# A decoder layer of 32 tiles on one core: second buffers for the front's packs, small scales on GpSimd, TensorE kept busy ahead of the weights, and new instruction orders

## The chip, the cores and the metric

One NeuronCore of a Trainium2 chip runs the kernel. The metric is the device time of one execution in microseconds (us); the number to compare is the median of several executions. TensorE (PE in the profile) multiplies, VectorE (DVE), ScalarE (ACT) and GpSimd (POOL) do the rest, and the sync engine (SP) issues the DMAs. Each engine runs its own instruction list in order and waits for the others through semaphores.

## What is computed

The reference is one decoder layer on x of 32 x 128 x 256 with a context of the same shape, each of the 32 sequences being one tile:

```python
x = _layernorm(x + _L0_attn_ref(x, Wq, bq, Wk, bk, Wv, bv, Wo, bo, orf))
x = _layernorm(x + _L0_xattn_ref(ctx_1024, x, ctx_1024, xWk, xWq, xWv))
x = _layernorm(x + _L0_ffn_ref(x, w_gate, w_up, w_down))
```

The first attention is linear, with 16 heads of 16: phi(z) = (exp(z orf^T / 16^0.25 - |z|^2 / 8) + 1e-6) / 8, kv = phi(k)^T v, out = phi(q) kv / (phi(q) sum phi(k)), and then the output projection. The second is softmax attention of the tile's x over its context, with 16 x 16 matrices shared by the heads. The FFN (256 to 1024 to 256, silu gate) quantizes activations to 8 bits by row and weights to the three values -1, 0, 1 by matrix.

## The kernel before, in words

Every tile passes through about 70 steps, each a small function with the tile number t. A step waits for its producers, issues one to 32 instructions and counts up its own semaphore. The steps, in the order of the data:

- Front: load_x; xhi and xlo (GpSimd, L468 to L474) split x into two fp16 parts in xpk; xTp transposes them; xT copies them out of PSUM; qkm and vm project with passes of 512 and 256 columns (L1355); qk and v (VectorE, L969 to L981) add the biases; sq, nf, nr form the norms; hi (ScalarE, L676), lo (GpSimd, L501), nhi and nlo (L483 to L489) fill pkA, an fp16 pack that the DMA transposes qT and kT turn into pkAT; phq0, phq1, phk0, phk1 and the exponentials behind them give the features.
- Linear attention: kvs, vsm, kve, kvp, kvm, nump, nT, ntp, rd, at, aTp, aT, wo, ad1, and the layer norm bs1, y1, rs1, x1.
- Second attention: chi and clo pack the context in pkC, transposed by cT; x1Tp, x1T, tm, thi, tlo fill pkT, transposed by tT; s0 and s1 (L1587, L1596) give scores, m0 and m1 the row maxima, mTp, mT and the DMA `row` put them into the operand; st0, st1, p0, p1, pv0, pv1, oxT, oxp, rx, oxn, ya2 and the layer norm bs2, y2, rs2, x2.
- FFN: am, ac, ar, qnt, xqf quantize; xqTp, xqT, g0, g1, u0, u1; th0, th1, gl0, gl1, hu0, hu1, hh0, hh1, hx, hc, hr, hs scale; hm0, hm1, hq0, hq1 quantize, the DMA transpose hqT; dn, ad3, and the layer norm bs3, y3, rs3, ot, store.

A layer norm ends in `rstd` (L510) on GpSimd: ve, nm, a power, nmr, each on 128x1. `sg` (L1091) and `sd` (L1147) on VectorE form three scales of 128x1: sgate and sprod from acl, sdown from hcl.

The tiles are software-pipelined: in iteration i an engine issues each of its steps for tile i minus the step's lag. The order of the steps within an iteration is written out by hand for each engine, in `iteration(i, par)`; par is the parity of the tile and picks the buffer where there are two. `ramp` holds the same steps as tiles enter (each with its first index and the tile it stops at), with the preparation of the FFN weights in between (`once`), `drain` the same as tiles leave. Both are straight code; two iterations and then a compiled loop of two iterations per turn stand between them (`run`, L306), so that tiles 14 to 29 pass the front in the loop. Where two steps share a PSUM bank, a wait for an unrelated step (`wait_looped`, `only_at`) keeps them apart. xpk, xT, qk, pkA, pkAT, phk, x1T, pkC, pkT, hq and hqT have one buffer, which gives waits such as these:

```python
wait_ahead(pool, t, par, ("nr", 0), landings=(("kT", -1), ("qT", -1),))   # nhi, L484
wait_moved(act, "kT", t, par, -1)                                         # hi, L677
wait(dve, "lo", t, -1)                                                    # qk_, L972
```

The FFN weights are loaded by SP (load_gate, load_up, load_down, 1 MB each). `magnitudes` (L941) sums their absolute values on VectorE, `ffn_means` adds over the partitions on TensorE, `ffn_scales` and `scaled` (L958, L961) scale them, `signed` (L659) takes signs, and `transpose_ffn` and `evacuate_ffn` bring them into place.

Of the kernel before, what the change touches and what calls it, by code (L numbers as in the profile page):

```python
# [14 lines left out]
H = 16  # L15
# [14 lines left out]
def decoder_kernel(nc: bass.Bass, x, ctx_in, Wq, bq, Wk, bk, Wv, bv, Wo, bo, orf,  # L30
# [4 lines left out]
    with ExitStack() as stack:  # L35
# [6 lines left out]
        def sem(name):  # L42
# [73 lines left out]
        x1T = sb("x1T", [P, 2, P])  # L116

        pkT = sb("pkT", [P, H, 4, DK], F16)
        pkC = sb("pkC", [P, H, 4, DK], F16)
# [20 lines left out]
        th = sb("th", [P, 2, 512])  # L140
        g1 = sb("g1", [P, 2, 512])
# [8 lines left out]
        hq = sb("hq", [P, 2, 512], BF16)  # L150
        hqT = sb("hqT", [P, 8, P], BF16)
# [37 lines left out]
        at_ox = pb[1][:, :]
        at_kvT = pb[5][:, 0:4 * (M + 1)]  # L190
        at_t = pb[0][:, 0:256]
        at_phq1 = pb[4][:, :]
        at_aT = pb[7][:, 0:256]
        at_dn = pb[5][:, 0:256]
        at_xT = pb[2][:, 0:256]
        at_qk = pb[2][:, :]
        at_x1T = pb[5][:, 0:256]
        at_st0b = pb[2][:, :]

        at_prep = (pb[3][:, :], pb[3][:, :], pb[7][:, :], pb[4][:, :], pb[5][:, :], pb[7][:, :])  # L200
# [121 lines left out]
        def _(sp):  # L322
# [1599 lines left out]
```

## Time and profile before

| | |
|---|---|
| median of 3 executions | 497.37 us (496.7 to 497.66) |
| the profiled execution | 498.58 us, span from first to last instruction 496.5 us |
| mean granted TensorE clock | 0.965 |
| busy: TensorE, VectorE, ScalarE, GpSimd | 441.2, 435.8, 429.7, 393.8 us |
| share of the chain that ended last | TensorE 53%, DMA 14%, VectorE 9%, ScalarE 8%, GpSimd 6% |
| first and last start of ot, tiles 0 and 31 | 119.2 and 493.7 us |

The busy time is the sum over the engine's instructions. The span is 2.1 us shorter than the execution's own time. A wait in the profile is given as the idle time of an engine and the instruction that ended it.

### The profile page before, as it was taken

Reading aid. Unit: us, or ns where it says so; the run is one execution under the profiler, and the core shown is the slowest. Engines: PE = TensorE matmul, PEld = TensorE weight load, DVE = VectorE, ACT = ScalarE, POOL = GpSimd, SP = SyncE. Lnnn points to the kernel's source line nnn. Section 1 sums busy time; section 2 is a strip of 40 time slices with the busy share of each in tenths; the row PEclk is TensorE's granted clock in tenths of the full one; section 3 lists DMA queues with packets and bytes.
Section 4 is the critical chain, followed back from the end, with each engine's and each line's share of the span. In section 5 each row is a group of like instructions: output and inputs, shape, how many; then the busy total and the mean of one; then the engine's idle time right before and its main releaser. Section 6 shows DMA issues by size and latency. Waiting matters only on the chain.

```text
span 496.5 us, 18431 instructions
## 1 busy us (share of the span) xinstructions
PE 441.2 (89%) x6531; PEld 302.6 (61%) x6566; DVE 435.8 (88%) x1286; ACT 429.7 (87%) x879; POOL 393.8 (79%) x885
## 2 busy tenths in 40 slices
PE   5578898999999999999999999999999999877651
PEld 3245666767676766777767677777666666544310
DVE  7755568999999998999999999999999899898761
ACT  3298988999999998999999999999999999667532
POOL 3289677889997997999999999999998897664423
PEclk9899999999999999999999999999999999899765
DMA  7758577778887688566666666666777666633122
GB/s 203 252 119 141 122 120 113 133 128 140 140 141 144 126 139 150 115 143 139 145 145 140 139 140 146 142 139 142 148 147 136 114 140 126 110 62 66 47 33 63
DMA packets 192659, 64.27 MB, mean 129 GB/s; under 512 B 172384, under 2 KB 192352, under 8 KB 192608
## 3 DMA queue, kind: packets, MB, share of 16 engines
q1 hardware_dynamic: 192432, 63.60, 64.5%
q8 instruction: 30, 0.49, 0.4%
q14 instruction: 21, 0.17, 0.1%
q10 hardware_dynamic: 176, 0.01, 0.0%
HBM read 17.31 MB, written 4.19 MB: 43 GB/s over the span
## 4 chain that ended last, share of the span: by engine, by line
PE 53%; DMA 14%; DVE 9%; ACT 8%; issue 7%; POOL 6%; SPq 3%; POOLq 0%; DVEq 0%; ACTq 0%
PE bank L1355 8%; PE bank L1741 7%; DMA tT<-pkT 6%; PE bank L1780 4%; PE bank L1682 4%; PE bank L1543 4%; DMA hqT<-hq 4%; PE bank L1453 3%; PE bank L1500 2%; PE bank L1387 2%; DMA pkAT<-pkA 2%; PE bank L1719 2%; DVE hh L1101 2%; PE bank L1571 2%; PE bank L1515 2%
## 5 line engine op out<-in xcount | busy, mean ns | idle before, releaser
L1355 PE MATMUL bank<-wq_hi,xT 128*128 128x512 f16 (+1 forms) x256 | 72.2, 337 | 1.7 <-ACT xT L636 1.5
L516 POOL TENSOR_TENSOR rs<-ve,mhalf 128x1 f32<-128x1 f32 x96 | 53.3, 555 | 0.0
L1097 DVE SCALAR_TENSOR_TENSOR g<-th,bank 128x512 f32<-128x512 f32 x64 | 43.2, 674 | 6.3 <-ACT th L774 4.7
L1052 DVE TENSOR_REDUCE negm<-bank 128x4 f16<-128x512 f32 x64 | 42.7, 668 | 6.3 <-PE bank L1592 6.3
L750 ACT ACTIVATE pT<-bank 128x512 f32<-128x512 f32 x64 | 39.0, 610 | 8.5 <-PE bank L1672 7.4
L1780 PE MATMUL bank<-downT,hqT 128*128 128x256 bf16 x256 | 35.7, 286 | 9.0 <-DMA hqT<-hq 8.9
L1053 DVE TENSOR_REDUCE negm<-bank 128x4 f16<-128x512 f32 x64 | 43.4, 679 | 0.0
L682 ACT ACTIVATE x<-y,nmr,rs 128x256 f32<-128x256 f32 x64 | 39.8, 622 | 3.9 <-DVE y L1158 3.2
L1355 PE MATMUL bank<-wq_lo,xT 128*128 128x256 f16 (+1 forms) x128 | 43.0, 336 | 0.0
L1101 DVE TENSOR_TENSOR hh<-g,bank 128x512 f32<-128x512 f32 x64 | 42.3, 673 | 0.0
L702 ACT ACTIVATE phq<-bank 128x512 f32<-128x512 f32 x64 | 39.8, 639 | 2.6 <-PE bank L1387 2.6
L1104 DVE TENSOR_REDUCE hmax<-hh 128x1 f32<-128x512 f32 x64 | 40.5, 674 | 0.0
L751 ACT ACTIVATE pT<-bank 128x512 f32<-128x512 f32 x64 | 39.3, 614 | 0.0
L702 ACT ACTIVATE phk<-bank 128x512 f32<-128x512 f32 x64 | 38.1, 627 | 1.0 <-PE bank L1392 1.0
L1682 PE MATMUL bank<-pT,ctxv 128*32 128x128 f32 x1024 | 36.0, 276 | 2.9 <-ACT pT L751 2.9
L503 POOL TENSOR_TENSOR pkA<-qk,pkA 128x512 f16<-128x512 f32 x32 | 37.2, 1162 | 0.7 <-ACT pkA L636 0.7
L1355 PEld LDWEIGHTS bank<-wq_hi,xT 128*128 128x128 f16 x256 | 25.3, 99 | 19.7 <-issue 1.7
L512 POOL TENSOR_TENSOR ve<-mv,lneps 128x1 f32<-128x1 f32 x96 | 18.5, 193 | 23.0 <-DVE mv L1017 12.0
L1741 PE MATMUL bank<-gateT,xqT 128*128 128x512 bf16 x97 | 32.7, 407 | 4.2 <-ACT xqT L636 2.2
L498 POOL TENSOR_SCALAR phq<-phq 128x1024 f32<-128x1024 f32 x32 | 33.5, 1048 | 3.4 <-ACT phq L702 1.0
L1543 PE MATMUL bank<-woT,attT 128*128 128x256 f32 x128 | 36.2, 405 | 0.0
L1741 PE MATMUL bank<-upT,xqT 128*128 128x512 bf16 x124 | 35.9, 400 | 0.2
(184 smaller groups left out, 1574.3 us busy)
## 6 DMA issues: line engine op xcount, KB each, us to landing
xs<-in_x_dram SPq DMA_DIRECT2D x32, 128.0 KB, 2.3
xr<-in_x_dram SPq DMA_DIRECT2D x32, 128.0 KB, 2.3
cs<-in_ctx_dram SPq DMA_DIRECT2D x32, 128.0 KB, 2.2
out_dram<-ot SPq DMA_DIRECT2D x32, 128.0 KB, 2.0
ffn_ld<-in_L_ffn_w_gate_dram SPq DMA_DIRECT2D x1, 1024.0 KB, 10.0
ffn_ld<-in_L_ffn_w_up_dram SPq DMA_DIRECT2D x1, 1024.0 KB, 6.5
ffn_ld<-in_L_ffn_w_down_dram SPq DMA_DIRECT2D x1, 1024.0 KB, 8.6
pkAT<-pkA SPq DMA_TRANSPOSE x64, 3.2
```

The source lines that it names most:

```text
L516: g.tensor_tensor(rs[n - 1][:, :], ve[n - 1][:, :], mhalf[:, :], ALU.pow).then_inc(done[f"pw{n}"], 1)
L702: sc.activation(o, i.rearrange("p (c t) -> p c t", c=parts), ACT.Exp, scale=0.5).then_inc(done[name], 1)
L1052: v.tensor_reduce(negm[:, 0, cols], even.rearrange("p (c t) -> p c t", c=4), AX, ALU.max, negate=True)
L1053: v.tensor_reduce(negm[:, 1, cols], odd.rearrange("p (c t) -> p c t", c=4), AX, ALU.max, negate=True).then_inc(done[name], 1)
L1097: v.scalar_tensor_tensor(g1[:, n, :], th[:, n, :], 1.0, gate, ALU.add, ALU.mult).then_inc(done[f"gl{n}"], 1)
L1101: v.tensor_tensor(hh[:, n, :], g1[:, n, :], up, ALU.mult).then_inc(done[f"hu{n}"], 1)
L1104: v.tensor_reduce(hmax2[:, n:n + 1], hh[:, n, :], AX, ALU.max, apply_absolute_value=True).then_inc(done[f"hh{n}"], 1)
L1355: last = T.matmul(o, xT[:, 2 * part + c, :], w[:, c, cols], start=(n == 0), stop=(n == 5))
L1543: last = T.matmul(at_wo, attT[:, k, :], woT[:, k, :], start=(k == 0), stop=(k == 1))
L1682: last = T.matmul(at_pv[32 * j:32 * j + 32, q * P:(q + 1) * P], ctxv[:, par, h, :], pT[:, grp, odd, k, :], start=True, stop=True)
L1741: last = T.matmul(o, xqT[:, k, :], w[:, k, 512 * n:512 * n + 512], start=(k == 0), stop=(k == 1))
L1780: last = T.matmul(at_dn, hqT[:, k, :], downT[:, k, :], start=(k == 0), stop=(k == 7))
```

## The change

- xpk, xT, qk, pkA, pkAT, phk, x1T, pkC, pkT, hq and hqT get a second buffer, picked by the tile's parity; th and g1 move into the space of wld. The waits for the previous tile's use of these buffers go. Their clearing at the start covers only the slots that stay zero.
- `rstd` loses nm: nmr is one tensor-scalar instruction (mean x power x -1).
- sgate, sprod and sdown are formed on GpSimd; ad3 waits for sd.
- TensorE issues 18 matmuls of 128x128 on the identity before the first weight transpose, and 8 after the second.
- PSUM banks are assigned anew, and with them the waits that keep sharers apart.
- The orders of all five engines are new, in ramp, iteration and drain. In the ramp the sums of absolute values stand elsewhere: before, the gate's sum preceded tile 0's qk and the other two preceded tile 1's; now the gate's stands after v of tile 0 and before its nr, up's before qk of tile 1, down's between its qk and v; the means and the first scaling precede qk of tile 2. up and down are loaded right behind gate, Wo behind x of tile 2.

```diff
-        xpk = sb("xpk", [P, 2, D], F16)
-        xT = sb("xT", [P, 4, P], F16)
-        qk = sb("qk", [P, 2 * H, DK])
+        xpk = sb("xpk", [P, 2, 2, D], F16)
+        xT = sb("xT", [P, 2, 4, P], F16)
+        qk = sb("qk", [P, 2, 2 * H, DK])
...
+        pkA = sb("pkA", [P, 2, H, 4, 32], F16)
+        pkAT = sb("pkAT", [P, 2, H, P], F16)
...
+        phk = sb("phk", [P, 2, H, M + 1])
...
+        x1T = sb("x1T", [P, 2, 2, P])
...
+        pkT = sb("pkT", [P, 2, H, 4, DK], F16)
+        pkC = sb("pkC", [P, 2, H, 4, DK], F16)
...
-        th = sb("th", [P, 2, 512])
-        g1 = sb("g1", [P, 2, 512])
+        th = wld[:, 0:2, :, :].rearrange("p a b d -> p a (b d)")
+        g1 = wld[:, 2:4, :, :].rearrange("p a b d -> p a (b d)")
...
+        hq = sb("hq", [P, 2, 2, 512], BF16)
+        hqT = sb("hqT", [P, 2, 8, P], BF16)
...
-        at_xT = pb[2][:, 0:256]
-        at_qk = pb[2][:, :]
...
+        at_xT = pb[3][:, 0:256]
+        at_qk = pb[1][:, :]
...
             def load_r(t, par):
-                wait(sp, "xb", t, -2)
...
             def qT(t, par):
-                wait_ahead(sp, t, par, ("lo", 0), ("phq0", -1))
...
+                wait_ahead(sp, t, par, ("lo", 0), ("nlo", 0))
...
-                once(load_output, i, -109)
...
+                once(load_down, i, -137)
...
+                lead(load_x, i, -137, 16)
+                once(load_gate, i, -162)
...
+                once(load_up, i, -147)
...
+                once(load_output, i, -135)
...
             def xhi(t, par):
-                wait_ahead(pool, t, par, ("xTp", -1), landings=(("x", 0),))
...
+                wait_ahead(pool, t, par, landings=(("x", 0),))
...
             def nhi(t, par):
-                wait_ahead(pool, t, par, ("nr", 0), landings=(("kT", -1), ("qT", -1),))
...
+                wait_ahead(pool, t, par, ("nr", 0))
...
-                g.tensor_tensor(nm[n - 1][:, :], mv[n - 1][:, par, 0:1], mone[:, :], ALU.mult)
                 wait(pool, f"ve{n}", t)
                 g.tensor_tensor(rs[n - 1][:, :], ve[n - 1][:, :], mhalf[:, :], ALU.pow).then_inc(done[f"pw{n}"], 1)
-                wait(pool, f"pw{n}", t)
-                g.tensor_tensor(nmr[n - 1][:, :], nm[n - 1][:, :], rs[n - 1][:, :], ALU.mult).then_inc(
-                    done[f"rs{n}"], 1)
+                wait_ahead(pool, t, par, (f"pw{n}", 0))
+                g.tensor_scalar(nmr[n - 1][:, :], mv[n - 1][:, par, 0:1], rs[n - 1][:, :], -1.0, ALU.mult,
+                                ALU.mult).then_inc(done[f"rs{n}"], 1)
...
+            def sg(t, par):
+                first_time(pool, t, 0, scales, 5)
+                g.tensor_tensor(sgate[:, par:par + 1], acl[:, :], cgate[:, :], ALU.mult)
+                g.tensor_scalar(sprod[:, par:par + 1], acl[:, :], cprod[:, :], acl[:, :], ALU.mult,
+                                ALU.mult).then_inc(done["sg"], 1)
+
+            def sd(t, par):
+                g.tensor_tensor(sdown[:, par:par + 1], hcl[:, :], cdown[:, :], ALU.mult).then_inc(done["sd"], 1)
...
             def hi(t, par):
-                wait_moved(act, "kT", t, par, -1)
-                wait_moved(act, "qT", t, par, -1)
-                copy(pkA[:, :, 0:3:2, :], qk_pairs.unsqueeze(2).to_broadcast([P, H, 2, 32]), "hi")
+                copy(pkA[:, par, :, 0:3:2, :], qk_pairs[par].unsqueeze(2).to_broadcast([P, H, 2, 32]), "hi")
...
             def oxT_(t, par):
                 wait(act, "pv0", t)
-                wait(act, "pv1", t)
...
-            v.memset(pkA[:, :, :, :], 0.0).then_inc(cleared, 1)
+            v.memset(pkA[:, :, :, 3, :], 0.0).then_inc(cleared, 1)
...
-                wait(dve, "lo", t, -1)
...
             def ad1(t, par):
                 wait(dve, "wo", t)
-                wait(dve, "xb", t)
...
-            def sg(t, par):
-                v.tensor_scalar(sgate[:, par:par + 1], acl[:, :], cgate[:, :], None, ALU.mult)
-                v.tensor_scalar(sprod[:, par:par + 1], acl[:, :], cprod[:, :], acl[:, :], ALU.mult,
-                                ALU.mult).then_inc(done["sg"], 1)
...
-            def sd(t, par):
-                v.tensor_scalar(sdown[:, par:par + 1], hcl[:, :], cdown[:, :], None, ALU.mult)
...
             def ad3(t, par):
                 wait(dve, "dn", t)
+                wait(dve, "sd", t)
...
+            def keep_busy(count):
+                for _ in range(count):
+                    T.matmul(at_qk[:, 0:P], idh[:, :], idh[:, :], start=True, stop=True)
+
+            keep_busy(18)
             for n in range(3):
                 transpose_weight(n, weight_banks[n])
+                if n == 1:
+                    keep_busy(8)
```

The new order of an iteration, each step with its lag:

```
SP: qT 2, cT 5, kT 2, load_x 0, hqT 9, load_c 3, row 6, store 11, load_r 3, tT 5

GpSimd: sd 9, phe 3, rs3 10, xhi 0, xlo 0, nf 1, rs2 7, nhi 1, lo 1, nlo 1, clo 4, xb 3, chi 3, qnt 7, xqf 7, rs1 4, hq1 8, hq0 8, sg 7, ya2 6

ScalarE: vh 6, kvm 3, thi 5, xT 0, nT 3, p1 6, p0 6, x2 7, ephk1 2, oxT 6, ephk0 2, hm1 8, ephq1 2, hm0 8, xqT 7, sq 0, ot 10, ephq0 2, th0 7, x1 4, mT 5, th1 7, x1T 4, hi 0

VectorE: aT 4, gl1 8, hu0 8, hu1 8, tlo 5, nr 1, ad3 9, hh1 8, hh0 8, ad1 4, hx 8, bs1 4, bs3 9, hc 8, y1 4, y3 9, am 7, rd 3, ac 7, hr 8, ar 7, hs 8, m0 5, at 3, qk 0, rx 6, oxn 6, m1 5, vsm 2, bs2 6, kve 2, v 0, gl0 7, y2 6

TensorE: dn 9, xTp 0, nump 3, st1 6, st0 6, wo 4, phk1 2, ntp 3, phk0 2, pv1 6, pv0 6, s0 5, phq1 2, qkm 0, oxp 6, xqTp 7, phq0 2, s1 5, kvs 2, g0 7, vm 0, mTp 5, g1 7, vhp 5, u0 7, x1Tp 4, kvp 2, aTp 3, u1 7, tm 4
```

## Rows read from the trace of the kernel before

**Rows 1.** Busy time of each engine in stretches of the span (us, instruction counts).
```profile
0.00:20.00 20.00, 10.12 (x39) 5.60 (x40) 13.26 (x31) 5.93 (x9) 6.19 (x28) 0.96 0.83 260
...
220.00:240.00 20.00, 19.95 (x323) 14.18 (x325) 19.70 (x63) 19.92 (x43) 18.54 (x44) 1.00 0.66 147
...
440.00:460.00 20.00, 14.12 (x173) 7.96 (x173) 17.64 (x56) 14.91 (x30) 9.53 (x26) 0.91 0.43 74
```

**Rows 2.** Chain of waits in the loop: start us, us, engine and line.
```profile
249.11 1.40 PE bank L1355 x6
...
262.05 1.40 PE bank L1355 x6
```

**Rows 3.** Groups of POOL instructions, ten tiles of the loop: busy, mean ns | idle before.
```profile
L514 POOL TENSOR_TENSOR nm<-mv,mone 128x1 f32<-128x1 f32 x30 | 5.8, 194 | 0.0
L518 POOL TENSOR_TENSOR nmr<-nm,rs 128x1 f32<-128x1 f32 x30 | 5.7, 192 | 2.4
L547 POOL TENSOR_SCALAR xm<-x,arec 128x256 f32<-128x256 f32 x10 | 4.8, 482 | 0.0
...
L552 POOL TENSOR_SCALAR xq<-xm 128x256 bf16<-128x256 f32 x10 | 4.1, 408 | 0.0
...
L485 POOL TENSOR_SCALAR pkA<-nrm 128x32 f16<-128x32 f32 x10 | 3.5, 345 | 3.8 <-DVE nrm L985 1.9 <-issue 1.9
```

**Rows 4.** Groups of DVE instructions, the same ten tiles.
```profile
L1093 DVE TENSOR_SCALAR sprod<-acl,cprod 128x1 f32<-128x1 f32 x10 | 2.6, 262 | 0.0
...
L1092 DVE TENSOR_SCALAR sgate<-acl,cgate 128x1 f32<-128x1 f32 x10 | 2.0, 202 | 0.0
...
L1148 DVE TENSOR_SCALAR sdown<-hcl,cdown 128x1 f32<-128x1 f32 x10 | 1.2, 120 | 0.0
```

**Rows 5.** DVE in order of time, start of the kernel: start us, us, line, operation.
```profile
12.50 0.19 DVE L939 TENSOR_TENSOR wvp<-wv_a,wv_b 128x32 f16<-128x32 f32 x1
14.68 2.29 DVE L943 TENSOR_REDUCE wsum<-ffn_ld 128x1 f32<-128x2048 f32 x1 [1.99 <-DMA ffn_ld<-in_L_ffn_w_gate_dram]
16.89 0.68 DVE L973 SCALAR_TENSOR_TENSOR qk<-bank,bqkv 128x512 f32<-128x512 f32 x1
...
19.06 0.42 DVE L985 TENSOR_REDUCE nrm<-qk2h 128x32 f32<-128x256 f32 x1 [1.17 <-POOL qk2h L493]
...
23.79 0.68 DVE L973 SCALAR_TENSOR_TENSOR qk<-bank,bqkv 128x512 f32<-128x512 f32 x1
...
29.35 0.69 DVE L973 SCALAR_TENSOR_TENSOR qk<-bank,bqkv 128x512 f32<-128x512 f32 x1 [1.77 <-POOL pkA L503]
```

**Rows 6.** PE in order of time, the first projection.
```profile
10.53 0.58 PE L1355 MATMUL bank<-wq_hi,xT 128*128 128x512 f16 x1 [0.78 <-ACT xT L636]
10.91 0.63 PE L1355 MATMUL bank<-wq_lo,xT 128*128 128x512 f16 x1
11.34 1.06 PE L1355 MATMUL bank<-wq_hi,xT 128*128 128x512 f16 x2
```

**Rows 7.** PE in order of time, the same projection in the loop.
```profile
249.27 0.38 PE L1355 MATMUL bank<-wq_lo,xT 128*128 128x512 f16 x1
249.48 0.59 PE L1355 MATMUL bank<-wq_hi,xT 128*128 128x512 f16 x2
```

**Rows 8.** Waits over the whole span: us in total, times, longest.
```profile
DVE qk L973 <- POOL pkA L503: 7.6, 11, 2.4
```

**Rows 9.** Busy time of each engine after the start, while tiles enter.
```profile
15.00:20.00 5.00, 1.62 (x7) 0.65 (x8) 3.83 (x5) 2.06 (x3) 1.43 (x3) 0.84 1.00 380
...
30.00:40.00 10.00, 8.04 (x152) 5.55 (x152) 6.86 (x14) 9.79 (x16) 8.47 (x11) 1.00 0.81 118
```

**Rows 10.** SP queue in order of time, one transpose in the loop.
```profile
257.74 1.23 SPq L365 DMA_TRANSPOSE tT<-pkT  x1
```

**Rows 11.** PE in order of time, the first score matmul of that tile.
```profile
261.66 0.23 PE L1591 MATMUL bank<-cT,tT 64*128 64x128 f16 x1
```

**Rows 12.** DMA issues of the page: KB each, median us from issue to landing.
```profile
pkAT<-pkA SPq DMA_TRANSPOSE x64, 3.2
```

More of the change, by code:

```diff
@@ L880, in _ @@
+                trail(oxT_, i, -37, 24)
+                trail(ephk1, i, -41, 28)
+            run(act, ramp, iteration, drain, (-30, -15), 16, 30, (-13, 0))
         @block.vector
@@ L1189, in ramp @@
-                once(magnitudes[0], i, -22)
-                lead(y2, i, -11, 6)
-                lead(v_, i, -17, 12)
-                lead(gl0, i, -10, 5)
-                lead(aT, i, -14, 9)
-                lead(hu0, i, -10, 5)
-                lead(gl1, i, -10, 5)
-                lead(tlo, i, -13, 8)
-                lead(hu1, i, -10, 5)
-                once(scales_of[2], i, -14)
-                once(scales_of[1], i, -15)
-                once(feature_weights, i, -26)
-                lead(ad3, i, -9, 4)
@@ new lines, in ramp @@
+                lead(gl0, i, -15, 5)
+                lead(gl1, i, -15, 4)
+                lead(aT, i, -19, 8)
+                lead(hu1, i, -15, 4)
+                lead(hu0, i, -15, 4)
+                lead(tlo, i, -18, 7)
+                lead(hh1, i, -15, 4)
+                lead(ad3, i, -14, 3)
+                once(magnitudes[0], i, -22)
+                once(scales_of[1], i, -19)
+                lead(hh0, i, -15, 4)
+                lead(hx, i, -15, 4)
+                lead(nr, i, -22, 11)
@@ new lines, in ramp @@
+                once(scales_of[2], i, -18)
+                lead(hc, i, -15, 4)
+                lead(ad1, i, -19, 8)
+                lead(bs3, i, -14, 3)
+                lead(bs1, i, -19, 8)
+                lead(rd, i, -20, 9)
+                lead(y1, i, -19, 8)
+                lead(am, i, -16, 5)
+            def iteration(i, par):
+                go(aT, i, par, 4)
+                go(gl1, i, par, 8)
+                go(hu0, i, par, 8)
+                go(hu1, i, par, 8)
+                go(tlo, i, par, 5)
+                go(nr, i, par, 1)
+                go(ad3, i, par, 9)
+                go(hh1, i, par, 8)
+                go(hh0, i, par, 8)
+                go(ad1, i, par, 4)
+                go(hx, i, par, 8)
+                go(bs1, i, par, 4)
+                go(bs3, i, par, 9)
+                go(hc, i, par, 8)
+                go(y1, i, par, 4)
+                go(y3, i, par, 9)
+                go(am, i, par, 7)
+                go(rd, i, par, 3)
@@ L1285, in _ @@
+            run(dve, ramp, iteration, drain, (-29, -10), 14, 30, (4, 16))
         @block.tensor
@@ L1354, in project @@
                     for part, w in ((0, wq_hi), (0, wq_lo), (1, wq_hi)):
-                        last = T.matmul(o, xT[:, 2 * part + c, :], w[:, c, cols], start=(n == 0), stop=(n == 5))
+                        last = T.matmul(o, xT[:, par, 2 * part + c, :], w[:, c, cols], start=(n == 0), stop=(n == 5))
                         n += 1
@@ new lines, in ramp @@
+                lead(phk0, i, -30, 10)
+                lead(phk1, i, -30, 10)
+                if i == -27:
+                    pe.wait_ge(ffn_out, 2)
+                once(ternaries[3], i, -27)
+                lead(ntp, i, -29, 9)
+                if i == -25:
+                    pe.wait_ge(done["ad1"], 4)
+                once(ternaries[4], i, -25)
+                lead(pv1, i, -26, 6)
+                lead(pv0, i, -26, 6)
+                lead(s0, i, -27, 7)
+                lead(phq1, i, -30, 10)
@@ L1889, in drain @@
[L1889 to L1898 removed]
+                trail(pv1, i, -36, 24)
+                trail(xTp, i, -42, 30)
```

1100 lines of the change are left out of this document (510 added, 590 removed), and 4 rows, old and new, of the table done.

## The prediction

> **What bounds the kernel now.** I read the stretches first, then the chain of waits in the loop, then the start in order of time, and last the groups of small instructions. In the stretches the reader is to see three regimes [rows 1]. In the first 20 us no engine is full: TensorE is busy 10.12 us of 20, ScalarE 5.93. In the loop four engines are nearly full at once: 19.95, 19.70, 19.92 and 18.54 of 20. While the last tiles leave, VectorE leads with 17.64 of 20 and TensorE has 14.12. Busy shares can't say which of three full engines sets the pace, so I go to the chain: between one tile's first projection and the next it stays on TensorE, from 249.11 to 262.05 us [rows 2]. The period is 12.94 us, and TensorE's instruction stream fills it. GpSimd is the only one with visible slack there: it sits idle 3.8 us in ten tiles before the norm pack's first half (L485), 0.38 us per tile [rows 3], so its own work is 12.94 - 0.38 = 12.56 us.
>
> **The change, part by part.**
>
> TensorE in the loop. The matmuls are the same in number and shape, and the new order keeps the same neighbours where the shape of the array use changes (scores after a full-width matmul, value weights before scores, features before s1). So the period of 12.94 us stays, a term of 0, with 0.1 us per tile either way as its bound; 16 tiles go through the compiled loop, 1.6 us.
>
> Work taken off VectorE. sgate, sprod and sdown cost it 202, 262 and 120 ns [rows 4], 0.58 us per tile. In the loop TensorE covers all of it: nothing. Without that cover, in the drain, it would be worth 0.58 us for each of the last five tiles, but those also wait for transposes and ScalarE; I take 0.5 us, between 0 and 2.9.
>
> Work put on GpSimd. The layer norm drops three nm instructions, 3 x 194 = 582 ns [rows 3]. nmr turns from tensor-tensor at 192 ns into tensor-scalar with a pointer; the trace has no such form at one element. The pointer's price is read from xm against xq: 482 - 408 = 74 ns [rows 3], so three nmr gain 222 ns. sgate and sdown are tensor-tensor of the shape of nm, 194 ns each; sprod has two pointers, 194 + 2 x 74 = 342. Sum: 222 + 730 - 582 = +0.37 us per tile, against 0.38 us of slack: GpSimd just stays under TensorE, a term of 0. From below: nmr unchanged and sprod at VectorE's 262 gives 650 - 582 = +0.07. From above: each of the nmr and sprod at the 345 ns of L485, the nearest tensor-scalar (32 elements, written with a stride), gives 3 x 153 + 345 + 388 - 582 = +0.61, and half of the 3.8 us is put down to issue, which may not be slack at all: 0.61 - 0.19 = 0.42 over, 6.7 us over 16 tiles. I stay with the middle because the row nearest in form is the pointer one.
>
> The start. Tile 0's q/k result is on VectorE at 16.89 us, and it stood behind the absolute sum of the gate weights (14.68 us, 2.29 us long, itself waiting for its DMA) [rows 5]. In the new ramp that sum comes after qk and v of tile 0. The projection started at 10.53 with passes 0.38 and then 0.43 us apart [rows 6], so six are done by 13.1, and qk can start at 13.2. nr of tile 0 is then behind the sum, at 17.0 instead of 19.06. Of the two other sums only one now stands ahead of qk of tile 1: 17.3 + 2.29 = 19.6 instead of 23.79. The third takes until 22.5; the mean, its small chain and the first scaling (1.3 us) bring qk of tile 2 to 25.1 instead of 29.35 [rows 5]. Gain so far: **4.2 us**. It needs the up weights by 17.3 and x of tile 2 by about 20. The up and down loads stood behind x of tiles 2 and 3 and now go right behind gate, so x of tile 2 queues behind 2 MB. The DMA engines were full from 15 to 20 us at 380 GB/s [rows 9], so 2 MB take 5.5 us after gate's landing at 14.7, and x lands at about 20: just in time. Bound: up to 2 us of the gain lost.
>
> Second buffers. qk waited for the previous tile's low pack (POOL L503) 7.6 us in 11 waits [rows 8]. 1.77 us of that is at 29.35 and counted. Its cover is thin only between 30 and 45 us: ScalarE is already busy 9.79 and GpSimd 8.47 of 10 there [rows 9], so most of the room is taken. Of the remaining 5.8 us I credit **1.3**, between 0 and 4. The waits of GpSimd for the pack's transposes go the same way and are inside this term. xpk of tile 1 no longer waits for tile 0's transposes; that is hidden behind the sums.
>
> TensorE kept busy. 26 small matmuls stand before and between weight transposes that wait for DMA, so they delay nothing. The first projection ran at 0.43 us from pass to pass of 512 columns, against 0.21 in the loop [rows 6, 7], so TensorE was at its 1.2 GHz level there and is at 2.4 in the loop; from 15 to 20 us the granted clock still averaged 0.84 [rows 9]. At full speed six passes end at 11.9, but VectorE is busy with feature weights until 12.7 [rows 5], so qk gains at most 0.5 us, and the sum behind it takes that away again: 0. That the small matmuls don't lift the clock at all would therefore cost the same nothing.
>
> Fewer memsets, packs cleared in one slot only: about 1 us of VectorE before 6 us, hidden behind the weights' DMAs. Removed waits (xb, pv1) cost nothing where the order already implies them.
>
> **Sum.** 4.2 + 1.3 + 0.5 = 6.0 us off the profiled execution's 498.58, 492.6. The median of the runs shown is 497.37, 1.2 lower, so the forecast for the median is **491.4**. About 0.2% (1 us) is what a measurement can tell from no change.
>
> **The rivals.**
> 1. GpSimd becomes the bound in the loop (slower). sg now stands behind both hq instructions, and th0 on ScalarE waits for it; sd stands before ad3. If all six forms cost 345 ns, GpSimd gains 3 x 153 + 3 x 345 - 582 = 0.91 us, 0.53 over the slack; 16 tiles give 8.5, the sum turns to 498.58 - 6.0 + 8.5 = 501.1, median 499.9. It decides from +0.755 us per tile on (6.0 / 16 + 0.38). For it: the slack is 0.38. Against: one-element tensor-tensors cost 194 ns. Chance 0.12. The Trainium skill, GPSIMD Engine Reference, section 4.1 Engine selection, advises VectorE for elementwise work and puts GpSimd at about twice the time for two-input operations. By that rule the three moved ones would cost 2 x 584 = 1168 ns in place of 730, GpSimd would be 0.43 over its slack, and the median 498.3. The trace speaks against it at this size: 194 ns on GpSimd beside 120 to 202 on VectorE.
> 2. The order makes one transfer late. tlo now follows gl1, hu0 and hu1 on VectorE. The tT transpose was issued at 257.74 and s0 started at 261.66 [rows 10, 11], 3.9 us for a landing of 3.2 [rows 12]: 0.7 us of room. VectorE has spare time to be early, but a delay of 1.0 us would stop TensorE 0.3 us in each of some 28 tiles, 8.4 us: 499.8. Chance 0.11.
> 3. The early gain is given back: tiles enter sooner but the middle is as full as before, or x of tile 2 is late. Then only about 1 us is left: 496.5. Chance 0.13.
> 4. More than I count: the new drain order may also keep TensorE busier, which has 20 - 14.12 = 5.9 us idle in 440 to 460 us alone [rows 1]. Half of that, and as much again in the stretch behind it, is 6 us more: 485.4. Against it: the last tiles are a serial chain of one tile's steps, which no order shortens. Chance 0.16.
> 5. The forecast, 488 to 494.5. Chance 0.48.
>
> **How the numbers follow.** Faster: all of 5 and 4, and half of 3, 0.70. Same: the other half of 3, 0.07. Slower: 1 and 2, 0.23. The low end, 484, takes in 4 with 1.5 us of the bounds; the high end, 499, takes in 3, the upper bound of GpSimd and the mild half of 1 and 2.
>
> **What would show it.** In the changed profile: the first three qk starts at about 13, 20 and 25 us; no wait of qk for the low pack; the loop's chain still on TensorE with 12.94 us from tile to tile; GpSimd nearly without idle but not on the chain; the projection passes of tile 0 about 0.21 us apart. I am wrong if the period is over 13.1, if the chain in the loop goes through GpSimd or the tT transpose, or if qk of tile 2 is not before 27.

## The result and the profile after

The changed kernel takes 507.08 us (median of 3 runs, 507.08 to 507.38), the kernel before 497.37. The ratio is 1.0201 (95% interval 1.0169 to 1.0232): it is slower by 2.0%, where 491.4 us and faster was forecast. The profiled execution has a span of 505.3 us; the one before had 496.5.

The same three stretches as [rows 1], columns as there (PE, PEld, DVE, ACT, POOL busy us; granted clock; DMA share; GB/s):

```profile
0.00:20.00 20.00, 11.01 (x74) 7.47 (x74) 14.36 (x33) 6.01 (x10) 7.49 (x30) 0.88 0.85 267
220.00:240.00 20.00, 19.62 (x319) 13.83 (x318) 18.64 (x57) 19.20 (x41) 18.35 (x41) 1.00 0.63 130
440.00:460.00 20.00, 14.84 (x174) 8.73 (x175) 18.03 (x46) 13.82 (x30) 12.26 (x32) 1.00 0.41 73
```

In the loop VectorE, ScalarE and TensorE have all become a little less busy and none more. Such a row can't say who sets the pace: GpSimd's busy share has not risen either (18.54 before, 18.35 now). The chain of waits says it. On the page, its shares of the span by engine:

```profile
POOL 32%; ACT 16%; PE 14%; issue 13%; DMA 12%; DVE 10%; SPq 1%; POOLq 1%; ACTq 0%; DVEq 0%
```

The distance between the starts of qk of one tile and of the next, by which all kernels are compared here, is 13.67 us in the loop in place of 12.94. It is the forecast's own sign of being wrong: a period over 13.1 and the chain through GpSimd. GpSimd in order of time (start us, us, line, operation, idle before and what ended it), with the pieces of one tile:

```profile
252.15 0.49 POOL L545 TENSOR_SCALAR xm<-x,arec 128x256 f32<-128x256 f32 x1
252.79 0.41 POOL L550 TENSOR_SCALAR xq<-xm 128x256 bf16<-128x256 f32 x1 [0.15 <-POOL xm L545]
...
255.55 0.19 POOL L554 TENSOR_TENSOR sgate<-acl,cgate 128x1 f32<-128x1 f32 x1
255.73 0.34 POOL L555 TENSOR_SCALAR sprod<-acl,cprod 128x1 f32<-128x1 f32 x1
256.02 0.73 POOL L506 TENSOR_TENSOR y<-ox,x 128x256 f32<-128x256 f32 x1
256.71 0.19 POOL L559 TENSOR_TENSOR sdown<-hcl,cdown 128x1 f32<-128x1 f32 x1
256.98 1.05 POOL L497 TENSOR_SCALAR phq<-phq 128x1024 f32<-128x1024 f32 x1
258.11 0.19 POOL L511 TENSOR_TENSOR ve<-mv,lneps 128x1 f32<-128x1 f32 x1
258.38 0.56 POOL L514 TENSOR_TENSOR rs<-ve,mhalf 128x1 f32<-128x1 f32 x1
259.12 0.27 POOL L516 TENSOR_SCALAR nmr<-mv,rs 128x1 f32<-128x1 f32 x1 [0.18 <-POOL rs L514]
259.34 0.41 POOL L468 TENSOR_SCALAR xpk<-xs 128x256 f16<-128x256 f32 x1
```

Read the starts, not the durations. The layer-norm group takes 259.34 - 258.11 = 1.23 us from its start to that of the next instruction. The durations of its three instructions add up to only 1.02; the rest is time in which each waits for the one before. And GpSimd has no slack left: from 200 to 340 us its longest idle time is the 0.18 us before nmr. In the kernel before it still had some, in front of the norm pack (GpSimd in order of time, that kernel):

```profile
259.70 0.68 POOL L543 TENSOR_TENSOR pkC<-cs,pkC 128x256 f16<-128x256 f32 x1
260.75 0.34 POOL L485 TENSOR_SCALAR pkA<-nrm 128x32 f16<-128x32 f32 x1 [0.37 <-issue]
261.17 0.35 POOL L489 TENSOR_TENSOR pkA<-nrm,pkA 128x32 f16<-128x32 f32 x1
```

The norm pack starts 1.05 us behind pkC there, where two starts behind such an instruction are else 0.64 apart: 0.41 us a tile of slack. Over ten tiles of the changed kernel the groups of instructions show the waiting for nmr, next to xm, xq and the moved three (compare [rows 3], where nmr had 192 ns and 2.4 us of idle):

```profile
L516 POOL TENSOR_SCALAR nmr<-mv,rs 128x1 f32<-128x1 f32 x30 | 8.0, 267 | 5.3 <-POOL rs L514 5.3
...
L550 POOL TENSOR_SCALAR xq<-xm 128x256 bf16<-128x256 f32 x10 | 4.1, 407 | 1.5 <-POOL xm L545 1.5
...
L555 POOL TENSOR_SCALAR sprod<-acl,cprod 128x1 f32<-128x1 f32 x10 | 3.4, 339 | 0.0
...
L559 POOL TENSOR_TENSOR sdown<-hcl,cdown 128x1 f32<-128x1 f32 x10 | 1.9, 194 | 0.0
L554 POOL TENSOR_TENSOR sgate<-acl,cgate 128x1 f32<-128x1 f32 x10 | 1.9, 193 | 0.0
```

At the start the forecast came true. VectorE in order of time, the rows that answer to [rows 5]:

```profile
11.42 0.69 DVE L983 SCALAR_TENSOR_TENSOR qk<-bank,bqkv 128x512 f32<-128x512 f32 x1
...
14.19 2.29 DVE L954 TENSOR_REDUCE wsum<-ffn_ld 128x1 f32<-128x2048 f32 x1 [1.75 <-DMA ffn_ld<-in_L_ffn_w_gate_dram]
...
19.10 0.68 DVE L983 SCALAR_TENSOR_TENSOR qk<-bank,bqkv 128x512 f32<-128x512 f32 x1
...
26.36 0.69 DVE L983 SCALAR_TENSOR_TENSOR qk<-bank,bqkv 128x512 f32<-128x512 f32 x1 [1.73 <-PE bank L1356]
```

qk of tiles 0, 1, 2 starts at 11.42, 19.10 and 26.36 us (13.2, 19.6 and 25.1 forecast; 16.89, 23.79, 29.35 before). Where the time then goes is seen tile by tile, in starts of qk and of ot (us; the two right columns are experiments told below):

| | before | after | both edits back | the same, old start |
|---|---|---|---|---|
| qk, tile 4 | 45.57 | 40.47 | 40.68 | 42.70 |
| qk, tile 14 | 171.89 | 171.69 | 171.31 | 174.93 |
| ot, tile 0 | 119.25 | 118.05 | 118.49 | 121.41 |
| ot, tile 8 | 229.51 | 227.62 | 225.06 | 228.96 |
| ot, tile 18 | 358.86 | 364.32 | 354.88 | 358.73 |
| ot, tile 31 | 493.71 | 502.49 | 488.80 | 492.41 |

The changed kernel is 1.9 us ahead at ot of tile 8, 5.5 us behind at tile 18 and 8.8 us behind at the end.

### The profile page after: what moved, and what is told of

The parts are those of the page before. It is cut to its first block, busy times and chain, and to the rows that moved or that the text cites. A ratio compares the mean times of both kernels' runs of the same rounds, so it can differ in the third digit from the quotient of the medians.

```text
span 505.3 us, 18323 instructions
## 1 busy us (share of the span) xinstructions
PE 447.5 (89%) x6592; PEld 306.8 (61%) x6592; DVE 427.7 (85%) x1190; ACT 430.6 (85%) x879; POOL 409.2 (81%) x885
## 4 chain that ended last, share of the span: by engine, by line
POOL 32%; ACT 16%; PE 14%; issue 13%; DMA 12%; DVE 10%; SPq 1%; POOLq 1%; ACTq 0%; DVEq 0%
DMA tT<-pkT 7%; POOL rs L514 5%; POOL phq L497 4%; PE bank L1686 2%; DMA ffn_ld<-in_L_ffn_w_up_dram 2%; DMA hqT<-hq 2%; POOL xpk L472 2%; PE bank L1356 2%; ACT phk L713 2%; ACT pT L763 2%; POOL hq L563 2%; POOL xb L477 2%; POOL hq L567 2%; ACT hm L798 2%; POOL ve L511 2%
## 5 line engine op out<-in xcount | busy, mean ns | idle before, releaser
L1356 PE MATMUL bank<-wq_hi,xT 128*128 128x512 f16 (+1 forms) x256 | 70.6, 332 | 2.1 <-ACT xT L649 2.1
L1061 DVE TENSOR_REDUCE negm<-bank 128x4 f16<-128x512 f32 x64 | 43.8, 684 | 10.1 <-PE bank L1564 9.8
L1101 DVE SCALAR_TENSOR_TENSOR wld<-wld,bank 128x512 f32<-128x512 f32 x64 | 43.3, 678 | 4.6 <-ACT wld L785 3.8
L1062 DVE TENSOR_REDUCE negm<-bank 128x4 f16<-128x512 f32 x64 | 43.6, 680 | 0.0
L1108 DVE TENSOR_REDUCE hmax<-hh 128x1 f32<-128x512 f32 x64 | 41.6, 675 | 0.0
L1686 PE MATMUL bank<-gateT,xqT 128*128 128x512 bf16 x128 | 40.3, 402 | 1.0 <-ACT xqT L649 1.0
L1686 PE MATMUL bank<-upT,xqT 128*128 128x512 bf16 x128 | 38.9, 396 | 2.4 <-DVE wld L1101 0.2
L1105 DVE TENSOR_TENSOR hh<-wld,bank 128x512 f32<-128x512 f32 x64 | 40.9, 679 | 0.0
L516 POOL TENSOR_SCALAR nmr<-mv,rs 128x1 f32<-128x1 f32 x96 | 25.6, 267 | 16.8 <-POOL rs L514 16.8
## 6 DMA issues: line engine op xcount, KB each, us to landing
ffn_ld<-in_L_ffn_w_down_dram SPq DMA_DIRECT2D x1, 1024.0 KB, 13.2
```

Of the source, the lines that this page charges most:

```text
L1061: v.tensor_reduce(negm[:, 0, cols], even.rearrange("p (c t) -> p c t", c=4), AX, ALU.max, negate=True)
L1062: v.tensor_reduce(negm[:, 1, cols], odd.rearrange("p (c t) -> p c t", c=4), AX, ALU.max, negate=True).then_inc(done[name], 1)
L1101: v.scalar_tensor_tensor(g1[:, n, :], th[:, n, :], 1.0, gate, ALU.add, ALU.mult).then_inc(done[f"gl{n}"], 1)
L1105: v.tensor_tensor(hh[:, n, :], g1[:, n, :], up, ALU.mult).then_inc(done[f"hu{n}"], 1)
L1108: v.tensor_reduce(hmax2[:, n:n + 1], hh[:, n, :], AX, ALU.max, apply_absolute_value=True).then_inc(done[f"hh{n}"], 1)
L1356: last = T.matmul(o, xT[:, par, 2 * part + c, :], w[:, c, cols], start=(n == 0), stop=(n == 5))
```

## The experiments

Twelve kernels ran. "Period" is the mean distance of qk's starts from tile 20 to tile 28 in the profiled execution; the ratio is to the kernel before. A span is that of one profiled execution, and executions of one kernel spread by up to 5 us: the profiled one of "both back, scales early" is the fastest of its twelve (493.3 us, median 495.5), that of the kernel before stands 1.2 us above its median. So the ratios say more than the spans.

| kernel | ratio (95% interval) | span us | period us |
|---|---|---|---|
| changed kernel | 1.0201 (1.0169 to 1.0232) | 505.3 | 13.67 |
| layer-norm group back | 1.0098 (1.0071 to 1.0125) | 498.9 | 13.32 |
| scales back on VectorE, late | 1.0045 (1.0022 to 1.0067) | 500.9 | 13.25 |
| both back, scales late | 1.0074 (1.0042 to 1.0107) | 498.8 | 13.25 |
| both back, scales early | 0.9940 (0.9915 to 0.9965) | 491.6 | 12.98 |
| scales back on VectorE, early | 0.9967 (0.9943 to 0.9991) | 492.5 | 13.05 |
| changed, gaps filled | 1.0027 (1.0003 to 1.0051) | 497.5 | 13.04 |
| before, group changed | 1.0061 (1.0025 to 1.0097) | 498.4 | 13.07 |
| before, scales moved | 1.0150 (1.0114 to 1.0185) | 501.9 | 13.31 |
| both back early, no busy TensorE | 0.9934 (0.9910 to 0.9957) | 492.9 | 12.98 |
| both back early, x of tile 2 first | 0.9971 (0.9949 to 0.9992) | 492.1 | 12.98 |
| both back early, one-slot waits | 1.2090 (1.2032 to 1.2147) | 596.9 | 18.04 |
| both back early, old start | 1.0012 (0.9991 to 1.0033) | 495.2 | 12.98 |

**Which edit on GpSimd costs it.** First the layer-norm group as it was:

```diff
                 g.tensor_tensor(ve[n - 1][:, :], mv[n - 1][:, par, 1:2], lneps[:, :], ALU.add)...
+                g.tensor_tensor(nm[n - 1][:, :], mv[n - 1][:, par, 0:1], mone[:, :], ALU.mult)
                 wait(pool, f"ve{n}", t)
                 g.tensor_tensor(rs[n - 1][:, :], ve[n - 1][:, :], mhalf[:, :], ALU.pow)...
-                wait_ahead(pool, t, par, (f"pw{n}", 0))
-                g.tensor_scalar(nmr[n - 1][:, :], mv[n - 1][:, par, 0:1], rs[n - 1][:, :], -1.0, ...
+                wait(pool, f"pw{n}", t)
+                g.tensor_tensor(nmr[n - 1][:, :], nm[n - 1][:, :], rs[n - 1][:, :], ALU.mult)...
```

> The changed kernel with the layer-norm group on GpSimd as it was (nm back in its place, nmr a tensor-tensor again); everything else stays changed. My theory now: GpSimd sets the loop's period of 13.67 us, and the group without nm is longer, not shorter: 1.22 us from start to start in the changed trace against 1.07 in the trace before, because nm had stood in the time in which the power waits for ve, and nmr now waits for the power with nothing to do. Then three groups give back 0.46 us a tile: a period of 13.2 us, and some 7 us off the 507.1, about 500. Rival: the three moved scales alone cost the time and the group is as good as forecast (-0.36 us per tile); then putting it back makes the period 14.0 and the time 512. Second rival: GpSimd isn't the bound, a wait of the new order is; then nothing moves, 507.

Measured: 1.0% off the changed kernel's time, a period 0.35 us shorter. That is less than the 0.46 expected: 0.10 of it returns as a longer distance before xm (0.70 us behind pkC in place of 0.60). With one instruction more, the group is shorter. GpSimd in order of time in this kernel:

```profile
257.22 0.19 POOL L511 TENSOR_TENSOR ve<-mv,lneps 128x1 f32<-128x1 f32 x1
257.37 0.19 POOL L513 TENSOR_TENSOR nm<-mv,mone 128x1 f32<-128x1 f32 x1
257.51 0.56 POOL L515 TENSOR_TENSOR rs<-ve,mhalf 128x1 f32<-128x1 f32 x1
258.14 0.19 POOL L517 TENSOR_TENSOR nmr<-nm,rs 128x1 f32<-128x1 f32 x1
258.30 0.41 POOL L468 TENSOR_SCALAR xpk<-xs 128x256 f16<-128x256 f32 x1
```

1.08 us from 257.22 to 258.30, against 1.23. nm starts 0.15 us behind ve and the power 0.14 behind nm, 0.29 behind ve in all; without nm the power starts 0.27 behind ve. nm cost next to nothing, since it stood in the time in which the power waits for ve. And nmr starts 0.63 us behind the power here, 0.74 in the changed kernel.

Then the three scales back on VectorE, at what I took for their old places:

```diff
-                go(sd, i, par, 9)          # GpSimd
-                go(sg, i, par, 7)          # GpSimd
                 go(rx, i, par, 6)
+                go(sd, i, par, 8)
...
                 go(vsm, i, par, 2)
+                go(sg, i, par, 7)
```

> The changed kernel with sgate, sprod and sdown back on VectorE, at the places that they had in its order before; the layer-norm group stays changed. My theory: they take 0.75 us a tile of GpSimd (the forecast's 0.73 was right), so the period falls from 13.67 to where TensorE bounds it, 12.93 to 13.0 us, and the time by 11 to 12 us, to about 495. Rival (a wait of the new order or the new PSUM places set the period): no change on 507. Rival (VectorE has no room for 0.58 us more in the new order): the period stays over 13.3, above 501.

And both together:

> Both edits on GpSimd taken back, so what is left of the change is the second buffers, the new orders, the weights' loads and the busy TensorE. My theory: TensorE sets the period again, 12.93 us, and the 2.6 us won by tile 7 stay to the end: 494 to 496, the same as with the scales alone back within 1 us. Rival: the start's gain is given back in the drain (the last tile took 2.9 us more in the changed trace): 497 to 498, no faster than the kernel before.

Here my theory fell in part. Both kernels stop at a period of 13.25 us, far under 13.67 but 0.3 over TensorE's 12.94, and are no faster than the kernel before. The waits of the second one, from 225 to 330 us (engine, operand and line, what it waited for: us in total, times, longest):

```profile
PEld bank L1540 <- ACT x L679: 6.4, 8, 0.8
DVE attT L1033 <- PE bank L1521: 4.5, 8, 0.6
ACT wld L771 <- DVE sprod L1088: 3.2, 8, 0.4
```

The rows are one chain, read from below: ScalarE's first tanh waits 0.4 us in every tile for sprod, x1 of the layer norm is queued behind the tanh on ScalarE, TensorE's transposes of x1 wait for that, and VectorE for TensorE. In the changed order sgate and sprod stand on GpSimd behind hq; behind vsum on VectorE they come too late for that tanh. So the next kernel has them right behind arec:

```diff
                 go(ar, i, par, 7)
+                go(sg, i, par, 7)
...
                 go(vsm, i, par, 2)
-                go(sg, i, par, 7)
```

> As the kernel with both edits taken back, but with sgate and sprod right behind arec on VectorE and not behind vsum, where I had put them. With them behind vsum the period was 13.25 us, and in its trace the gate's tanh on ScalarE waits 0.4 us a tile for sprod (3.2 us in 8 waits), with x1 of the layer norm queued behind it and TensorE's transposes of x1 behind that (6.4 us in 8 waits). Theory A: that wait, an artefact of my place, is all that holds the period above TensorE's 12.94; then the period is 12.9 to 13.0, the time about 4 us less, 496 to 498. Theory B: the new orders themselves cost 0.3 us a tile (the cycle through VectorE, ScalarE and TensorE is longer in them); then the period stays at 13.2 or more and the time near 501.

Theory A holds: a period of 12.98 us and 0.9940 (median 495.5 us, a little under the 496 to 498 expected). The page's chain has 1% of GpSimd left:

```profile
DVE 34%; PE 31%; DMA 12%; ACT 11%; issue 8%; SPq 2%; POOL 1%; DVEq 0%; POOLq 0%; ACTq 0%
```

This version is 0.6% faster than the kernel before and beats both. Against the changed kernel the two edits on GpSimd are worth 2.0% + 0.6%, 13 us.

> The changed kernel with sgate, sprod and sdown back on VectorE, sgate and sprod right behind arec; the layer-norm group on GpSimd stays changed. Theory: GpSimd is relieved of the 0.75 us a tile that the three took (0.18 + 0.30 + 0.28 from start to start), 13.67 - 0.75 = 12.92 us of work with its gaps, just under the 12.98 us that the kernel with both edits taken back has; so the period is 13.0 to 13.1 and the time 496 to 498, close to that kernel. Then either edit alone would about fit, and both together don't. Rival: the group's gaps cost more in this order than their sum, a period over 13.2 and 499 or more.

With the scales early on VectorE and the changed group left in place the period is 13.05 and the ratio 0.9967 (median 495.7 us), close to what the theory had. In the new orders the changed group alone just fits (13.05), the moved scales alone don't quite (13.32), and the two together give 13.67.

**The same edits put into the kernel before.**

> The kernel before with one edit alone: nm left out of the layer-norm group and nmr a tensor-scalar of three inputs. My theory: the group becomes 0.15 us longer, 0.46 us a tile, against 0.38 us of slack of GpSimd of which half may not be slack: 0.1 to 0.3 us a tile over, 1.5 to 5 us more, 499 to 502. The forecast's account (an instruction less is 0.36 us a tile less): GpSimd gets more slack, no change on 497.4. Rival (slack is larger than shown): no change too, but with the group's spacing at 1.22 us in the trace, not below 1.07.

> The kernel before with one edit alone: sgate and sprod on GpSimd behind the second half of hq, sdown right behind them. Theory: GpSimd has about 0.4 us of slack in 12.94 (0.41 us behind pkC's low part) and gets 0.61 to 0.75 us: a period of 13.1 to 13.3 us and 500 to 503 us. Rival: its slack is 0.7 us (12.94 less 12.21 at the least spacing of each instruction), so the period stays under 13.0 and the time at 498.

In the kernel before, the changed group alone costs 0.6% (a period of 13.07 from 12.94, so an instruction less, which gives nmr its new form, made the kernel slower), and the moved scales alone 1.5% (13.31). The first lies within the theory's periods, the second 0.01 us above them, and its 504.1 us (median) just above its 500 to 503. Of GpSimd's 0.41 us in the kernel before, not all could be used: 0.46 us added gave a period 0.13 longer, and the scales' 0.61 (0.14 + 0.17 + 0.30 by starts) gave 0.37 longer, so that 0.33 and 0.24 us a tile were taken up.

**Is it the gaps or the instructions?**

```diff
-                go(sd, i, par, 9)
                 go(phe, i, par, 3)
-                go(rs3, i, par, 10)
+                go(ve3, i, par, 10)
+                go(sd, i, par, 9)
+                go(pw3, i, par, 10)
                 go(xhi, i, par, 0)
+                go(rs3, i, par, 10)        # now nmr alone
...
                 go(qnt, i, par, 7)
+                go(ve1, i, par, 4)
                 go(xqf, i, par, 7)
-                go(rs1, i, par, 4)
+                go(pw1, i, par, 4)
+                go(rs1, i, par, 4)         # now nmr alone
```

> The changed kernel with no instruction of GpSimd's loop added or left out, only placed anew: sdown between ve and the power of the third layer norm, the first half of x's pack between that power and nmr, ve of the first layer norm between xm and xq. Theory: what costs is the time in which an instruction waits for the one right before it (0.13 us behind ve, 0.08 behind the power, 0.195 between xm and xq), so the period falls from 13.67 by 0.13 + 0.08 + 0.13 + 0.19 = 0.5 us at most, to 13.2 or the bound that the orders set (13.25), and the time from 507 to about 500. Rival: the durations count, as the forecast had it: then nothing moves, 13.67 and 507.

With the same instructions as the changed kernel, three of them in other places, the period falls to 13.04 and the ratio from 1.0201 to 1.0027, some 9 us. That is more than the 0.5 us a tile expected. Behind the power alone 0.31 us are saved where 0.08 was expected: the next start comes 0.20 us sooner, and nmr now also fills the wait between the two halves of x's pack, another 0.11. GpSimd in order of time:

```profile
255.50 0.19 POOL L510 TENSOR_TENSOR ve<-mv,lneps 128x1 f32<-128x1 f32 x1
255.64 0.19 POOL L565 TENSOR_TENSOR sdown<-hcl,cdown 128x1 f32<-128x1 f32 x1
255.79 0.56 POOL L515 TENSOR_TENSOR rs<-ve,mhalf 128x1 f32<-128x1 f32 x1
256.32 0.40 POOL L468 TENSOR_SCALAR xpk<-xs 128x256 f16<-128x256 f32 x1
256.70 0.26 POOL L519 TENSOR_SCALAR nmr<-mv,rs 128x1 f32<-128x1 f32 x1
...
263.01 0.48 POOL L551 TENSOR_SCALAR xm<-x,arec 128x256 f32<-128x256 f32 x1
263.46 0.19 POOL L510 TENSOR_TENSOR ve<-mv,lneps 128x1 f32<-128x1 f32 x1
263.65 0.40 POOL L556 TENSOR_SCALAR xq<-xm 128x256 bf16<-128x256 f32 x1
```

sdown stands between ve and the power, which starts 0.29 us behind ve as with nm: it fills the place that nm had left. The next independent instruction starts 0.53 us behind the power, where nmr, which needs its result, had started 0.74 behind. And xq starts 0.19 us behind ve, 0.64 behind xm, no later than without ve between them.

**What is the start worth?**

```diff
+                once(magnitudes[0], i, -22)
                 once(magnitudes[1], i, -21)
+                once(magnitudes[2], i, -21)
...
                 lead(qk_, i, -22, 12)
```

(and the two lines taken out where they stood, behind v and oxn.)

> The kernel with both edits taken back and sg early (495.45 us), with the three absolute sums of the weights at the old places of VectorE's order: the first ahead of qk of tile 0, the other two ahead of qk of tile 1. The forecast's term: qk of tiles 0 to 2 comes 4 to 5 us later (16.9, 23.8, 29 us) and the end 4.2 us later, 499.7. Rival, for which the traces speak so far (ahead by 5 us at tile 4, by 1 to 2 us at tile 8, by none at tile 14): the gain is given back before the loop, and the end moves by less than 1 us, 496.5 or less.

VectorE in order of time in this kernel:

```profile
16.04 0.68 DVE L969 SCALAR_TENSOR_TENSOR qk<-bank,bqkv 128x512 f32<-128x512 f32 x1
...
22.94 0.68 DVE L969 SCALAR_TENSOR_TENSOR qk<-bank,bqkv 128x512 f32<-128x512 f32 x1
...
28.01 0.69 DVE L969 SCALAR_TENSOR_TENSOR qk<-bank,bqkv 128x512 f32<-128x512 f32 x1 [0.47 <-PE bank L1356]
```

The rival falls, and with it what I had read from the tiles. The old start costs 3.6 us at the end by the spans (495.2 and 491.6), and as much by the ratios (1.0012 and 0.9940, whose intervals don't overlap: 0.72%, 3.6 us, give or take 1.6). Only the places of the sums are old in this run; the loads and the small matmuls stay new, and its qk of tile 0 comes at 16.04 us, 0.85 ahead of the kernel before. The table above shows the 3.6 us whole from tile 14 on. A shrinking lead over the kernel before didn't mean a lost gain: by these single traces the new orders take longer to bring tiles in (with the old start qk of tile 14 is 3.0 us later than before) and less from there to the end of a tile (ot of tile 31 is 1.3 us earlier).

**The other parts.**

> The kernel with both edits taken back and sg early, without the 26 small matmuls ahead of the weights. The forecast's term for them is 0: the first projection's passes go back to 0.43 us from 0.21, qk of tile 0 comes up to 1.3 us later, behind which the absolute sum still waits for its DMA until 14.2; the time stays within 0.5 us of the same kernel with them. Rival: the later clock of the whole start depends on them; then 1 us or more is lost.

Without the 26 small matmuls the ratio is 0.9934 against 0.9940. The first projection on TensorE in order of time, first the kernel without them:

```profile
10.63 0.58 PE L1353 MATMUL bank<-wq_hi,xT 128*128 128x512 f16 x1 [0.78 <-ACT xT L635]
11.01 0.63 PE L1353 MATMUL bank<-wq_lo,xT 128*128 128x512 f16 x1
```

and with them:

```profile
9.42 0.38 PE L1356 MATMUL bank<-wq_hi,xT 128*128 128x512 f16 x1 [0.78 <-ACT xT L635]
9.63 0.38 PE L1356 MATMUL bank<-wq_lo,xT 128*128 128x512 f16 x1
```

Passes of 512 columns 0.21 us apart are the 2.4 GHz level, 0.43 apart (12.29 to 12.72 in the first kernel) 1.2 GHz. The matmuls do lift the clock, and qk of tile 0 comes 2.1 us earlier (11.33 against 13.46). Behind it the first absolute sum waits for its DMA, so that 0.7 us are left of it at qk of tiles 1 and 2 (18.66 against 19.39, 26.55 against 27.27), and the end doesn't move beyond the intervals, as forecast.

> The kernel with both edits taken back and sg early, with the load of the down weights issued behind x of tile 2 and Wo. In the changed trace its issue took 5.53 us at 6.15, so x of tile 2 was issued at 11.72 and GpSimd waited for it until 19.85. Theory of the late x: qk of tile 2 comes at 25 in place of 26.1 us, since x is there by 17. At the end: if the gain of the start reaches the end, up to 1 us less; if it is given back by tile 14, as in all kernels so far (5 us ahead at tile 4, 0 at tile 14), nothing, within 0.3 us. I expect nothing.

```diff
-                once(load_down, i, -137)
+                once(load_down, i, -134)
```

The end indeed did not get earlier (0.9971), but qk of tile 2 came at 27.00 us, not at 25. The SP queue and TensorE in order of time, the second fence TensorE's:

```profile
5.17 0.71 SPq L335 DMA_DIRECT2D ffn_ld<-in_L_ffn_w_up_dram  x1
5.93 5.15 SPq L350 DMA_DIRECT2D xs<-in_x_dram  x1
```

```profile
22.59 0.39 PE L1316 MATMUL bank<-wsum,onesf 128*128 128x3 f32 x2 [4.42 <-DVE wsum L940]
22.92 0.43 PE L1347 MATMUL bank<-idh,xpk 128*128 128x128 f16 x4
```

x of tile 2 is there at 17.2, where its pack begins, but TensorE has the mean of the weights ahead of its transposes and waits 4.42 us there for the third absolute sum. The run changed a second thing: the down weights landed later too, and the third sum, idle 1.02 us for them, started at 20.25 us in place of 19.26. So by itself it doesn't show what the late x costs. The changed kernel's own trace does: there tile 2's pack was ready at 21.0, and the mean of the weights, ahead of its transposes, stood on TensorE from 22.02 on. The late x was not what held tile 2.

> The kernel with both edits taken back and sg early (495.45 us), with four waits of the kernel before put back as if there were one buffer only: qk for the low pack of the tile before, hi and nhi for its two transposes, the transposes for the tile's features. The waits of x's pack and of the context's pack are not put back. The forecast credited the second buffers with 1.3 us, between 0 and 4. I expect 1 us more or less than that: 495.5 to 498; if the period rises over 13.05 the second buffers are worth more than the forecast's bound.

```diff
             def qk_(t, par):
                 first_time(dve, t, 0, b_in, 48)
+                wait(dve, "lo", t, -1)
...
             def hi(t, par):
+                wait_moved(act, "kT", t, par, -1)
+                wait_moved(act, "qT", t, par, -1)
```

(and likewise in nhi, qT and kT.) The median is 600.3 us, the period 18.04, far beyond what I expected. The waits from 300 to 400 us:

```profile
PEld bank L1760 <- DMA hqT<-hq: 20.7, 6, 3.7
...
ACT pkA L635 <- DMA pkAT<-pkA: 11.9, 6, 2.1
```

hi on ScalarE now waits up to 2.1 us for the transposes of the tile before, with all of ScalarE's list behind it, and the delay returns in everything queued behind. The run doesn't give the second buffers' worth in the old order: it shows that the new orders are built on them and can't be had without.

## Why the prediction was wrong

**The step that failed is GpSimd's term**, "222 + 730 - 582 = +0.37 us per tile, against 0.38 us of slack". By starts it is +1.15 us per tile against 0.41 of slack, and the rest is what the period grew by, 13.67 - 12.94 = 0.73. Its parts, as the mean distances of starts in the loop give them (before to after):

- The layer-norm group was credited with 582 - 222 = 0.36 us less per tile. It takes 0.15 us more each, 0.46 per tile: an error of 0.82 us. Two things were wrong. nm was priced at its duration of 194 ns, but starts stood 0.14 us apart, and that time would not have come free, because the power needs ve and, without nm, still starts 0.27 us behind it. And nmr, now needing the power's result with a pointer, waits 0.18 us idle for it and takes 267 ns, not 192: the price of the form was right (192 + 74), the wait behind the power was not in the sum. By starts nm's going is worth 0.04 us per tile where 0.58 was credited, and nmr costs 0.50 where 0.22 was. [Rows 3] held the sign of it, 2.4 us idle before nmr, which the prediction passed over.
- The moved three: 730 ns forecast, 0.18 + 0.30 + 0.28 = 0.75 measured. Right, with sprod at 339 ns for 342. By the Trainium skill, GPSIMD Engine Reference, section 4.1 Engine selection, a two-input operation takes about twice as long on GpSimd, an estimate of 2 x 584 = 1168 ns for the three. At 128x1 this trace doesn't agree: their durations add up to 726 ns. Its advice, to leave such work on VectorE, was right here for another reason: with them there the period is 12.98 us, so VectorE had the room and GpSimd had not.
- The order, for which the term had nothing: xq now stands right behind xm, 0.64 us from start to start in place of 0.45 with the low pack between them, +0.2. The low pack now stands between the two halves of the norm pack, of which the second needs the first: from the first half's start to the next one's it is 0.18 us in place of 0.43, -0.25.

**Rival 1** (GpSimd becomes the bound, chance 0.12) is what happened in its main point, and the price is near, 0.53 us over the slack forecast and 0.73 measured. But that is luck: it priced all six forms at 345 ns, while nmr took 267, sprod 339 and sgate and sdown 194; the rest of the price is waiting behind a producer, which it did not name. Its chance was too low because both bounds of the term were made of durations; the range to 499.0 took in +0.61 us and not the gaps. It also multiplied by 16 tiles. The two edits cost 13 us at 0.69 us a tile (13.67 - 12.98), 19 tiles' worth.

**Right in mechanism and size:** the start. 4.2 us forecast, 3.6 measured by taking it back. Its dates were less good. qk of tile 0 came 1.8 us before its forecast: the small matmuls were credited with at most 0.5 us there and gave 2.1, as the feature weights, which the forecast had on VectorE until 12.7, were done at 11.3. qk of tile 2 came 1.3 us after it: the mean of the weights ahead of tile 2 on TensorE was not seen, and the first passes behind it were 0.43 us apart again (24.17, 24.60 and 25.03 us), the 1.2 GHz level. **Right:** the busy TensorE at 0 for the end; the tT transpose (rival 2) does not stand in the loop's chain of the changed kernel (none between 157 and 434 us). **Rival 3** (the gain is given back) looked true tile by tile and is refuted, in the kernel with both edits back.

**The rest of the sum.** With both edits on GpSimd taken back the gain is 0.6% of the time, 3 us, where 6.0 was forecast (4.9 in the spans, 496.5 to 491.6, of which the two profiled executions exaggerate some). 3.6 are the start's. What is left, 1.3 us off the span and nothing that the ratio of 1.0012 can tell from 0, stands for the second buffers (1.3), the new drain and a loop of 12.98 us in place of 12.94. The runs don't part them, and the 0.5 us for VectorE's relief wasn't tried alone.

**Still open:** in the changed kernel ot of tile 31 comes 6.95 us behind ot of tile 30, before 4.09, with both edits back 6.43. So most of it belongs to what both kernels share, probably the new order of the drain (not shown), and not to the two edits on GpSimd. Ahead of tile 30's last matmuls the chain has

```profile
484.62 3.60 PE bank L1686 x8
488.21 1.71 PE bank L1757 x8
```

all four gate and up products of tile 31. No kernel with another drain was run.

## What to carry to other kernels

Price an instruction by the distance from its start to the next one's start, not by its duration, and ask what the next one needs: an independent instruction between a producer and its consumer on the same engine is nearly free as long as it fits into the consumer's wait, as nm did here, and taking it out gives next to nothing back. Where an engine is the bound, fill such gaps with work that is due anyway before taking work away. And a lead that shrinks against another kernel is no proof that a gain is lost: take the step back in the kernel itself and compare there.

## What the runs showed that was not expected

- GpSimd, 128x1: independent tensor-tensors of 190 to 194 ns start 0.14 us apart. A consumer right behind such a producer starts 0.27 us behind it; behind the power of 0.56 us it is 0.63 us for a tensor-tensor and 0.73 on the mean for a tensor-scalar with a pointer, while an independent instruction starts 0.53 behind. For 128x256, xq behind xm, it is 0.64 us, where an independent one starts 0.45 behind.
- In the new start the DMA right behind the gate and up loads (1 MB each) on SP's queue takes 5.15 us to issue, even if it is only the 128 KB of an x tile; in the changed kernel it was the down weights' 5.53. In the kernel before, where up and down were issued at 11.53 and 12.01 us, no DMA of the start took over 0.84 us to issue. What sets it is open.
- Where the scales stood on VectorE, 1.3% of the time hung on two instructions of 0.20 and 0.26 us (1.0074 against 0.9940), because a tanh on ScalarE waited for them with x1 queued behind it.
